# One kernel layer on eight cores: loads and stores of GpSimd's queue moved onto SyncE's queue, and one loop of weight loads reordered

## The reference

```
xn  = layernorm(x)                              # over 2048 features
# Mamba2 branch: rmsnorm, in_proj (2048 -> 10304), conv of width 4, rmsnorm, silu,
#                chunked state scan, rmsnorm, gate, out_proj (4096 -> 2048)
y   = mamba2(xn)                                # contains + xn as its own residual
h   = xn @ W1.T                                 # 2048 -> 8192
a   = gelu(clip(round(h / 0.1)) * 0.1)
out = x + y + a @ W2.T                          # 8192 -> 2048
```

## Time and profile before

| | us |
|---|---|
| median of the two runs | 6200.42 |
| the two runs | 5987.79 and 6413.05 |
| profiled execution, its time | 6005.77 |
| its span, slowest core (core 0) | 6004.2 |
| spans of the other cores | 5937.3 to 5991.3 |

### The profile page before, as it was taken

One profiled execution on the slowest core, in us unless ns is written; L12 is line 12 of the kernel. 1 busy time (PEld: TensorE's weight loads), 2 busy tenths in 40 slices (PEclk: granted clock), 3 DMA queues, 4 the chain that ended last, 5 costly groups with the idle time before them and its releaser, 6 DMA issues.

```text
span 6004.2 us, 60382 instructions; the slowest of 8 cores (5937.3 to 6004.2 us)
## 1 busy us (share of the span) xinstructions
PE 4404.1 (73%) x22744; PEld 2114.6 (35%) x22744; DVE 2377.2 (40%) x3525; ACT 1068.5 (18%) x1713; POOL 318.1 (5%) x257
## 2 busy tenths in 40 slices
PE   2069988888876768686867677777399769956888
PEld 0023333333332434343434344344144324422333
DVE  2866777731224646455555555555000000000111
ACT  4001111111113333333333333333000000000000
POOL 0000000000000000000000000000000000010000
PEclk7568999999996777777878777777699889978999
DMA  4443344444423232323232323231899789986544
GB/s 113 161 98 56 56 64 64 64 66 61 63 37 58 42 68 38 71 36 71 36 71 42 65 43 65 42 71 29 171 106 106 124 139 107 108 125 111 90 84 84
DMA packets 892718, 465.72 MB, mean 78 GB/s; under 512 B 757264, under 2 KB 839184, under 8 KB 884240
## 3 DMA queue, kind: packets, MB, share of 16 engines
q0 software_dynamic: 637616, 209.99, 32.1%
q1 hardware_dynamic: 254816, 251.87, 13.9%
HBM read 478.86 MB, written 142.61 MB: 104 GB/s over the span
## 4 chain that ended last, share of the span: by engine, by line
PE 67%; DVE 13%; ACT 7%; issue 6%; DMA 5%; SPq 2%; DVEq 0%; POOL 0%; ACTq 0%; POOLq 0%
PE pb L536 20%; PE pb L732 15%; PE pb L1258 14%; PE pb L1334 8%; SPq L84 2%; DVE arena L560 2%; PE pb L994 2%; PE pb L989 2%; DMA arena<-a_s 1%; DMA arena<-craw_s 1%; PE pb L992 1%; PE pb L991 1%; PE pb L990 1%; DVE arena L616 1%; ACT arena L943 1%
## 5 line engine op out<-in xcount | busy, mean ns | idle before, releaser
L536 PE MATMUL pb<-arena 128*128 128x512 bf16 (+1 forms) x5184 | 1194.9, 394 | 184.1 <-DVE arena L616 91.8
L1258 PE MATMUL pb<-arena 128*128 128x512 bf16 x4096 | 899.8, 382 | 236.3 <-DMA arena<-w2t 122.6
L732 PE MATMUL pb<-arena 128*128 128x512 bf16 x4096 | 957.6, 397 | 15.0 <-DVE arena L744 15.0
L536 PEld LDWEIGHTS pb<-arena 128*128 128x128 bf16 (+1 forms) x5184 | 517.0, 101 | 863.8 <-issue 388.6
L1258 PEld LDWEIGHTS pb<-arena 128*128 128x128 bf16 x4096 | 400.7, 98 | 735.2 <-issue 265.8
L732 PEld LDWEIGHTS pb<-arena 128*128 128x128 bf16 x4096 | 418.8, 103 | 553.4 <-issue 121.5
L1334 PE MATMUL pb<-arena 128*128 128x512 bf16 x2048 | 477.3, 398 | 184.3 <-DMA arena<-yg_s 104.2
L1281 DVE TENSOR_TENSOR arena<-pb,arena 128x512 f32<-128x512 f32 x64 | 41.3, 687 | 1092.8 <-PE pb L1258 1092.8
L1334 PEld LDWEIGHTS pb<-arena 128*128 128x128 bf16 x2048 | 206.9, 102 | 454.7 <-issue 235.8
L744 DVE TENSOR_SCALAR arena<-pb 128x512 f32<-128x512 f32 x256 | 177.1, 692 | 354.5 <-ACT arena L757 171.6
L989 PE MATMUL pb<-arena,id 64*128 64x128 bf16 x1024 | 265.3, 259 | 69.6 <-ACT arena L1013 69.6
(11 more groups left out here) (153 smaller groups left out, 4300.0 us busy)
## 6 DMA issues: line engine op xcount, KB each, us to landing
arena<-w2t POOLq DMA_DIRECT2D x32, 2048.0 KB, 28.1
arena<-w_in POOLq DMA_DIRECT2D x80, 512.0 KB, 7.1
arena<-w1t POOLq DMA_DIRECT2D x64, 512.0 KB, 8.6
a_s<-arena SPq DMA_DIRECT2D x64, 512.0 KB, 7.1
craw_s<-arena SPq DMA_DIRECT2D x48, 512.0 KB, 3.0
arena<-craw_s SPq DMA_DIRECT2D x32, 768.0 KB, 10.5
arena<-xT POOLq DMA_DIRECT2D x16, 1024.0 KB, 7.1
arena<-xT SPq DMA_DIRECT2D x16, 1024.0 KB, 6.4
```

What stands on the lines that cost most here:

```text
L536: last = e.matmul(pb[tb][0:w, :], wf[m % 2][:, k * w:(k + 1) * w], xn[k][:, tb * 512:(tb + 1) * 512], start=(k == 0), stop=(k == NK - 1))
L732: last = e.matmul(pb[idx % 2][:, :], w1b[m % 2][:, k * 128:(k + 1) * 128], xn[k][:, tb * 512:(tb + 1) * 512], start=(k == 0), stop=(k == N ...
L1258: last = e.matmul(pb[2 * (m % 2) + tb][:, :], w2slab[m % 2][:, k * 128:(k + 1) * 128], atile[k][:, tb * 512:(tb + 1) * 512], start=(k == 0 ...
```

## The change

In both passes over x and for the second part of the activations, GpSimd's DMAs move to SyncE, and the group gP goes. In the W2 stage the two loads of the activations stand ahead of the weight slabs in the text, and all weight slabs are issued in the m loop; in the second half (tb2 == 1) slabs 0 and 1 each wait for TensorE's count at that place in the list. For m = 1 this count holds the matmuls of m = 0 of the same half. The odd loads of `yg_s` stay on GpSimd, and take their semaphores from gG, the group of the weight slabs, in place of gP.

```diff
-        sc_cnt = []
         for k in range(NK):
-            if k % 2 == 0:
-                if k >= 2:
-                    p.w("sync", "sE", sc_cnt[k - 2])
-                sv = gS.issue("sync", xstage[k % 2][:, :], xT[k * 128:(k + 1) * 128, :])
-            else:
-                if k >= 2:
-                    p.w("gpsimd", "sE", sc_cnt[k - 2])
-                sv = gP.issue("gpsimd", xstage[k % 2][:, :], xT[k * 128:(k + 1) * 128, :])
+            if k >= 2:
+                p.w("sync", "sE", p.cnt["sE"] - 1)
+            sv = gS.issue("sync", xstage[k % 2][:, :], xT[k * 128:(k + 1) * 128, :])
...
-        p.w("gpsimd", "vE")
-        p.w("gpsimd", "sE")
         for k in range(NK):
-            if k % 2 == 0:
-                if k >= 2:
-                    p.w("sync", "vE", xcons[k - 2])
-                sv = gS.issue("sync", xstage[k % 2][:, :], xT[k * 128:(k + 1) * 128, :])
-            else:
-                if k >= 2:
-                    p.w("gpsimd", "vE", xcons[k - 2])
-                sv = gP.issue("gpsimd", xstage[k % 2][:, :], xT[k * 128:(k + 1) * 128, :])
+            if k >= 2:
+                p.w("sync", "vE", xcons[k - 2])
+            sv = gS.issue("sync", xstage[k % 2][:, :], xT[k * 128:(k + 1) * 128, :])
...
             p.o("vector", v_ln3, "vE")
+            p.w("sync", "vE")
             prs = []
-            if k % 2 == 0:
-                p.w("sync", "vE")
-                prs.append(gR.issue("sync", r_s[k], rstage[k % 2][:, :]))
-            else:
-                p.w("gpsimd", "vE")
-                prs.append(gP.issue("gpsimd", r_s[k], rstage[k % 2][:, :]))
+            prs.append(gR.issue("sync", r_s[k], rstage[k % 2][:, :]))
             rsems.append(prs)
         gR.waitall("sync")
-        gP.waitall("gpsimd")
...
-                p.w("gpsimd", "tE", p.cnt["tE"])
+            asem = [gS.issue("sync", ablock[:, 0:32, :], ...),
+                    gS.issue("sync", ablock[:, 32:64, :], ...)]
             w2sem, t5, v5 = [], [], []
-
-            def w2cast(m):
+            for m in range(NK):
+                if m >= 2:
+                    p.w("gpsimd", "tE", t5[m - 2])
+                elif tb2 == 1:
+                    p.w("gpsimd", "tE", p.cnt["tE"] - NK + m if False else 0) or \
+                        p.w("gpsimd", "tE")
                 ...
                 w2sem.append(gG.issue("gpsimd", dst_ap, src_ap))
-            w2cast(0)
-            w2cast(1)
-            asem = [gS.issue("sync", ablock[:, 0:32, :], ...),
-                    gP.issue("gpsimd", ablock[:, 32:64, :], ...)]
-            for m in range(NK):
-                if m >= 2:
-                    p.w("gpsimd", "tE", t5[m - 2])
-                    w2cast(m)
...
-            ygsems.append((gS if kf % 2 == 0 else gP).issue(
+            ygsems.append((gS if kf % 2 == 0 else gG).issue(
```

More of the change, by code:

```diff
@@ L246, in build @@
     gD = DGroup(p, "dD")
-    gP = DGroup(p, "dC")
     if n_phases >= 1:
@@ L315, in build @@
         p.w("tensor", "gE")
-        sc_cnt = []
         for k in range(NK):
-            if k % 2 == 0:
-                if k >= 2:
-                    p.w("sync", "sE", sc_cnt[k - 2])
-                sv = gS.issue("sync", xstage[k % 2][:, :],
-                              xT[k * 128:(k + 1) * 128, :])
-            else:
-                if k >= 2:
-                    p.w("gpsimd", "sE", sc_cnt[k - 2])
-                sv = gP.issue("gpsimd", xstage[k % 2][:, :],
-                              xT[k * 128:(k + 1) * 128, :])
+            if k >= 2:
+                p.w("sync", "sE", p.cnt["sE"] - 1)
+            sv = gS.issue("sync", xstage[k % 2][:, :], xT[k * 128:(k + 1) * 128, :])
             p.w("scalar", *sv)
@@ L334, in s_cast @@
                 return e.activation(sq_t[k % 2][:, :], xstage[k % 2][:, :], AF.Square)
-            sc_cnt.append(p.o("scalar", s_cast, "sE"))
+            p.o("scalar", s_cast, "sE")
             p.w("tensor", "sE")
@@ L1225, in build @@
                 p.w("sync", "tE", p.cnt["tE"])
-                p.w("gpsimd", "tE", p.cnt["tE"])
-            w2sem, t5, v5 = [], [], []
-            def w2cast(m):
+            asem = [gS.issue("sync", ablock[:, 0:32, :],
+                             a_s[0:32, :, tb2 * 1024:(tb2 + 1) * 1024]
+                             .transpose([1, 0, 2])),
+                    gS.issue("sync", ablock[:, 32:64, :],
+                             a_s[32:64, :, tb2 * 1024:(tb2 + 1) * 1024]
+                             .transpose([1, 0, 2]))]
+            w2sem, t5, v5 = [], [], []
+            for m in range(NK):
[4 more added lines that the diff above has]
+                        p.w("gpsimd", "tE")
                 src_ap = w2t[:, m * 128:(m + 1) * 128].rearrange(
```

## The result

The changed kernel is **2.5% slower**: ratio 1.0252, 95% interval 1.0186 to 1.0319, to the kernel before. Its runs took 6110.8 to 6157.4 us against 5982.9 to 5990.8; runs in which one die as a whole was over 1% slower than the other at a lower granted clock are left out of every ratio and count here, and lift the medians over all runs to 6426.9 and 6193.7. The forecast was +105 us (1.7%), within 2%, and 6070 to 6150 as the range. So +150 us stand against +105.

What follows compares the result with a forecast made beforehand. The bare second pass over x and the starts of the W2 halves were taken as the sensitive places; +111.6 - 2 - 5 + 0 = +105 us on 6005.8 gave 6110 us (+1.7%, within 2%), range 6070 to 6150.

Steps and rivals of the forecast that it cites:

- What bounds the kernel: Second pass over x lies bare on the path; in the W2 stage TensorE waits for loads at both halves' starts.
- Second pass: One queue holds load k+1 until slab k is done: 17.15 us per slab instead of 9.39, +116 us over 15 gaps.
- The two small gains: Second pass: first load has no second beside it, -1.1 us; first w_in slab is issued sooner and hidden, -3.5 us.
- First pass: First pass over x: all loads on SyncE, whose issue is shorter than GpSimd's; -2 us, bounds -5 and +4.
- W2 stage: Both halves: loads for m = 0 land sooner, second half's slab 1 is bare; 29 - 2g, taken as -5 us.
- g: W2 stage: gain at the start of each half from sooner loads for m = 0; 17 us taken, 12.5 to 26.
- the prediction's own case of 12.5: W2 stage, first half: slab 0 lands last of m = 0's three loads, so m = 0 gains only 12.5 us.
- The price of the bare slab: W2 stage, second half: slab 1, issued only after m = 0, makes m = 1 28.9 us longer.
- out_proj: Out-projection: odd yg loads wait on the weight slabs' semaphores but were issued about then anyway; 0 us, 2 either way.
- Starved slab 0: Rival, W2 stage: g goes to 0, stage costs +29, 6145 us; chance 0.29 together with loads of 8.4 us.
- Shorter loads: Rival, second pass: loads take 5.2 us as the cores' bursts come half as often; +78 us, 6083; chance 0.08.
- hidden loads: Rival, second pass: the queue doesn't hold the next load, so only the gains are left; 5994 us; chance 0.03.

Runs made afterwards that it cites:

- Both mended: Changed kernel, load k+1 queued ahead of slab k's wait and second-half slab 1 not waiting for m = 0; 1.0049 and 0.9941 of the kernel before (two chips).
- p2_only: Kernel before with only the second pass over x changed, all its loads and stores on SyncE; ratio 1.0199, runs of 6097 and 6104 us.
- a_sync: Kernel before with only the upper half of the activations moved to SyncE; ratios 0.9983 and 0.9947 on two chips; the run named here took 5988 us.
- W2 only: Kernel before with only the W2 stage's order of activations and slabs changed; ratios 1.0054, 0.9997 and 1.0008 on chips I, II and III.

## Why the prediction was wrong, point by point

The step that failed is the prediction's 0 us for the loops that the change does not touch: it took them at one granted clock for all cores and both kernels. In their place a pair of cores fell to 13/16 in out_proj and took some 45 us longer (core 2 573 us for m = 1 to 15, core 0 528), and that pair is the slowest. The +105 us added up from the parts that are touched hold for the median core.

- **What bounds the kernel.** Right: the second pass is bare, and the two starts of the W2 halves are the sensitive places.
- **Second pass.** Right in mechanism and size: 17.14 us per slab against 17.15, +115.6 us against +116, the landing of 6.8 us within what the earlier trace rows held. Picking the row with the same traffic around it, and not the 5.2 or 8.4 us of the earlier trace rows, made this exact. Both mended shows that it is the order, and p2_only that it comes alone.
- **The two small gains.** Right (-0.6 and -3.3 for -1.1 and -3.5).
- **First pass.** -4.7 for -2, at the edge of its bounds. Most of it is that the constants in front came in sooner: VectorE's first instruction ran at 34.7 us on the median core against 38.1. It goes with the first pass's change: in every kept trace with the old first pass it is at 37 to 38 us, in every one with the changed pass at 35 or 36. GpSimd's early load of slab 1 is no longer beside the constants, which the prediction counted only as a loss; that this load is the cause was not tested by itself.
- **W2 stage.** g was 8.9 in the first half and 15.2 in the second, where 17 stood. The size that was off is the guess that slab 0 lands somewhere between: it landed last on all eight cores, which is the prediction's own case of 12.5, and after 78 us in the median where 100.8 - 26 = 75 stood (69 to 84 us; on core 2 83.9, with the upper part at 80.5). The price of the bare slab was 22.9 for 28.9 on the median core (on core 2 it was the 29.5 it should be). The two misses cancel, which is luck: -1.2 against -5. Slab 0 as the last to land is what the Trainium skill's "DMA: Bandwidth & Descriptors" ("Queues, rings and completion order") leads to with its turns between queues; its +4 and the prediction's -5 lie on either side of the measured -1.
- **out_proj.** The order there cost +0.9. What the text had wrong is that nothing else could happen in it: on core 2 its m = 1 to 15 took 573 us for 529.6. This is the term that was left out; it is on no path of the change.
- **The sum.** Median core +95 us in the two profiled executions and +100 to +105 on chips II and III: the forecast's +105 is right for these and wrong by 50 us for the chip on which pairs fall. A second error hid in the base: the profiled execution before, 6005.8 us, held such falls itself. Its core 0, the slowest, had one in in_proj, as core 1, and core 4 did not; cores 2 and 3 had theirs in out_proj, as shown above:

```profile
361.00:653.00 292.00, 268.46 (x993) 105.71 (x992) 181.11 (x154) 26.77 (x14) 17.15 (x15) 0.80 0.35 53
...
361.00:653.00 292.00, 258.68 (x1166) 112.71 (x1188) 218.28 (x186) 30.86 (x17) 18.88 (x17) 1.00 0.42 62
```

  In the same 292 us the one loaded weights 992 times and the other 1188. The prediction made its sum from core 0 and never compared the cores' clocks by stage; that would have shown that pairs of cores lose 20 to 45 us in some stretch, that this was 0.3 to 0.7% of the time, and that the distance from +1.7% to 2% was smaller than that. The chance of 0.29 for over 2% had rivals from the loads only.
- **Rivals.** Starved slab 0: it did land last, but g was 12 us on average, and where no pair fell the changed W2 stage alone cost nothing (0.9997 and 1.0008 on chips II and III). Shorter loads and hidden loads: fell (6.8 us; 7.5 to 8.3 us of idle time at each slab, where 7.8 was forecast).

What stays open: why runs with the changed W2 stage on chip I had long falls in out_proj and those on two other chips did not, and whether they come from what the matmuls draw. The Trainium skill's "TensorE: Matmul & The Clock Gate" ("Seeing it yourself") knows the level of 13/16 as a limiter of peak current that takes a whole die, and says that all-zero operands don't trip it. That agrees with the level. On the extent the traces don't decide. In four kept executions (the changed kernel twice, both mended, and the a_sync run) two neighbouring cores had it and the die's other two had none anywhere; but the traces of the pairs have no time in common, so they don't say what those two were doing meanwhile.

In the kept execution of W2 only on chip III all four cores of die 1 had it, for 1075 to 1184 us each, in stretches between which the clock was back at its usual levels. On cores 4 and 5 the first ones begin 503, 810, 1142, 1423 and 1728 us from their start, on cores 6 and 7 at 2761, 3068, 3400, 3681 and 3986: each 2258 us later. Core 4 in one of them and just after:

```profile
810.00:970.00 160.00, 145.82 (x539) 57.98 (x549) 105.94 (x92) 15.91 (x9) 9.13 (x8) 0.81 0.34 53
970.00:1135.00 165.00, 145.95 (x659) 63.47 (x670) 125.61 (x109) 18.48 (x10) 11.42 (x10) 1.00 0.41 64
```

The simplest reading is that the whole die fell at once and that cores 6 and 7 had started 2258 us before cores 4 and 5. Then all of these falls lie within the time in which both pairs ran, or up to 44 us behind it. So a rival stands untested for the extra 50 us on chip I: how the executions of a die's two pairs lie against each other in time. No run here controlled it. Whether zeros avoid the falls no run here decides.

## What to carry to other kernels

A queue is a list in order: when a load is moved behind a wait that belongs to something else, two buffers become one, and the price per slab is what the buffer used to hide, here issue and landing, 7.75 us for each of 15 slabs, which can be read off the trace before. Put the next load ahead of that wait, and one queue does as well as two. Delaying a prefetch costs next to nothing (here a ratio of 1.0012) where the load in front of it gets the engines instead; ask what the freed bandwidth brings forward.

Before a sum is set against the slowest core, compare all cores stage by stage, at their granted clocks: the median core showed this change as 1.6 to 2.0% everywhere, while the slowest core's share depended on the chip.

## What the runs showed of the hardware

- The granted clock has a level of 13/16 besides full and half. In every kept trace that has it, both cores of a pair (0 and 1, 2 and 3, 4 and 5, 6 and 7) have it, and their first falls begin at the same time from each core's start to within 4 us (5716 us on cores 2 and 3 of the changed kernel). It ends and returns within a stage. Over m = 1 to 15 of out_proj it cost 37 to 66 us on top of 528, and about 20 where it lasted for the last part only (cores 2 and 3 of the kernel before).
- Long falls (a pair at a mean clock of 0.836 or less) came in 11 of 13 runs with the changed W2 stage on one chip, against 0 of 13 without, and in 2 of 32 on two others. Shorter ones don't show in the mean clock: 117 and 142 us at 13/16 left cores 2 and 3 of the kernel before at 0.844 and 0.841.
- With both parts on SyncE, where a core starts 16 MB of loads at once, the two cores of a pair were unequal: m = 0 of the first half ended 107 to 114 us after the scan on one and 118 to 122 on the other, where in the kernel before the two of a pair were within about 3 us of each other, at 122 to 133.
